# The shared network's second product in a vision transformer tower, formed transposed and turned back

## The chip, the cores and the metric

The kernel runs on one core of one Trainium2 chip. The metric is the device time in microseconds (us) of one execution; the kernel before was run three times: 559.74, 560.98 and 562.35 us, median 560.98.

## What is computed

64 images of 3 x 224 x 224 are cut into 8 x 8 patches; each patch (2352 numbers) becomes a token of 128 numbers, and each image has a class token beside its 64 patch tokens. One attention layer with 8 heads follows, then a feed-forward stage with two networks: a shared one, and eight experts of which two are chosen per token. All of it is in float32. The stage the change is about, cut to what matters:

```
flat = layernorm(h)                                  # tokens x 128
h_shared = swiglu(flat @ shared_in_w.T)              # tokens x 256
out_shared = h_shared @ shared_out_w.T + shared_out_b
h_expert = swiglu(flat @ expert_in_w.T)
routed = cnt @ expert_out_bias
for e in range(8):
    routed = routed + comb[:, e:e+1] * (h_expert @ expert_out_weight[e].T)
return h + (out_shared + routed)
```

## The kernel before

The images are worked on in eight groups of eight, so a group has 512 patch tokens (`TOK`), in four tiles of 128 (`TILES`). The 64 class tokens make one small group of their own at the end (`GROUPS`, 64 rows). Five programs, one for each engine, are written out by hand, and run in that order on their engine; they meet in semaphores (`need` waits for a count, `then_inc` adds to it). The order of the work is therefore the order of the code.

TensorE's body for group g does four things in turns. It runs the attention of group g; it multiplies out the patches of group g+1 into the PSUM bank `acc` (`fill`, L410, eighteen products with 128 rows and a last one, L415, with 48 rows); it turns the new tokens of g+1 into rows (`to_natural`, into bank C1); and it runs the feed-forward stage of group g-1 (`ffn_in`, `counts`, `shared_out`, `expert` 0 to 7). Groups 1 to 6 have all of this; group 0 has no group before it, and group 7 none after it, so that its body has an order of its own. After the eight bodies comes a tail: the feed-forward stage of group 7 (called L), and of the class tokens.

The shared network's second product for one tile of 128 tokens is `shared_out` (L564 to L577): the tile's columns of `hidden` are the stationary operand, the 128 columns of `w_sout` stream through, two such products (256 hidden numbers) are summed, and a third adds the biases (stationary `count_t`, 9 rows: eight expert counts and a one; streaming `out_bias`). The sum stands in bank C0 with tokens on the partitions. A float32 product is two instructions on TensorE in the trace, each with a weight load of its own.

In the body of groups 1 to 6 the order near it is: `prob_transpose(3)`, the last patches and L415, `shared_out` of tiles 0 and 1, `prob_v(3)` (the last product of the attention, L497), `to_natural`, `shared_out` of tiles 2 and 3, `expert` 0, `attn_transpose`, `expert` 1, `out_proj`, `expert` 2, `normed_t`, `expert` 3 to 5, `z_transpose` (L396 with z_nat), `expert` 6 and 7. `expert(g-1, 0)` writes bank C1 and waits for `nat_done`, which is ScalarE's copy of the new tokens out of C1. `z_transpose` waits for `z_done`, VectorE's last step of the second layernorm.

VectorE's body goes, from the end of `prob_v(3)` on: `attn_scale(1)` (L1099), `attn_sum(1)` (L1113), `norm1` of g+1 (L1004 to L1017; its power is done by GpSimd, L1442), `shared_add` (L1217, which waits for the shared product), `norm1_scale`, `weigh` 0, `residual` (L1119), `norm2` (power by GpSimd, L1446), `weigh` 1, `norm2_scale` (L1021, four instructions that write z_nat), and the other `weigh`s (L1233). ScalarE's body copies PSUM to SBUF (`probs_out`, `counts_out`, `natural`, `attn_out`, `normed_t`), all through the helper at L796.

## Time and profile before

| what | value |
|---|---|
| the runs | 559.74, 560.98, 562.35 us |
| span of the profiled execution | 562.2 us |
| its own time | not listed apart; the highest of the runs is 562.35 us |
| TensorE busy | 502.9 us, 89% of the span |
| weight loads busy | 353.4 us, 63% |
| VectorE busy | 335.3 us, 60% |
| ScalarE busy | 179.7 us, 32% |
| GpSimd busy | 183.0 us, 33% |
| TensorE's mean granted clock | 0.923 |

The span is the time from the first to the last instruction of one execution. TensorE is by far the busiest engine, but a busy share is an average over stages: what counts is the chain of waits, which starts at the last instruction and goes back at each step to what released it. In the profile's lists a matmul stands as out<-streaming operand, stationary operand; a line such as L396 or L796 is that of a helper, so that the tile's name says which step it is. The PEclk row of the page is the granted clock in 40 slices of 14 us, in tenths (9 is 90% or more).

### The profile page before, as it was taken

The numbers are of one execution on the slowest core, as the hardware profiler recorded it, in microseconds if no ns is written. First come the engines' busy times: TensorE is split into PE (matmuls) and PEld (weight loads), VectorE is DVE, ScalarE is ACT, GpSimd is POOL, SyncE is SP. The second block draws the span as 40 slices with busy tenths as digits, with TensorE's granted clock in tenths as the row PEclk, the third lists the DMA queues.
The fourth block names the chain that finished last, engine by engine and source line by source line (L and its number), as shares of the span: only waits on it lengthen the run. The fifth ranks groups of instructions, "written<-read, shape, count | busy, mean of one in ns | idle before, by whom it ended". The sixth has DMA issues, their size and how long they took to land.

```text
span 562.2 us, 7098 instructions
## 1 busy us (share of the span) xinstructions
PE 502.9 (89%) x2241; PEld 353.4 (63%) x2241; DVE 335.3 (60%) x867; ACT 179.7 (32%) x334; POOL 183.0 (33%) x214
## 2 busy tenths in 40 slices
PE   5596885999999999999999999999999968698775
PEld 2244543855875587558755876587658756596563
DVE  0042358274776477647764777577756768935672
ACT  0015215342174216421642164216421652002320
POOL 6000006221271128112811182118211825226235
PEclk9788696599999999999999999999999998758988
DMA  8954150036004510451045104510000000000000
GB/s 342 366 179 175 45 187 1 0 112 211 22 0 131 193 41 1 132 179 53 0 131 174 57 0 129 172 61 1 20 1 0 2 19 1 0 1 1 18 2 21
DMA packets 14413, 44.71 MB, mean 80 GB/s; under 512 B 1721, under 2 KB 7090, under 8 KB 14386
## 3 DMA queue, kind: packets, MB, share of 16 engines
q1 hardware_dynamic: 12882, 42.39, 22.6%
q10 hardware_dynamic: 1504, 1.99, 1.1%
q8 instruction: 14, 0.23, 0.2%
q14 instruction: 13, 0.11, 0.1%
HBM read 42.24 MB, written 2.13 MB: 79 GB/s over the span
## 4 chain that ended last, share of the span: by engine, by line
PE 65%; DVE 17%; issue 7%; DMA 4%; POOL 4%; ACT 1%; ACTq 1%; DVEq 0%; POOLq 0%; SPq 0%
PE acc L410 21%; PE scores L471 6%; PE O L497 5%; PE B L396 4%; DMA bq_row<-in_bq_row 3%; DVE z_nat L1021 3%; PE acc L629 2%; DVE stats L1004 2%; PE B L453 2%; PE acc L415 2%; PE C L547 1%; POOL rstd L1446 1%; PE C L574 1%; DVE attn_nat L1113 1%; PE scores L549 1%
## 5 line engine op out<-in xcount | busy, mean ns | idle before, releaser
L410 PE MATMUL acc<-x_main,w_patch 128*128 128x512 f32 x288 | 141.4, 619 | 5.9 <-DMA w_patch<-in_w_patch 5.9
L410 PEld LDWEIGHTS acc<-x_main,w_patch 128*128 128x128 f32 x288 | 54.7, 200 | 50.3 <-issue 42.0
L1509 POOL TENSOR_TENSOR prod<-prod 128x512 f32<-128x512 f32 (+1 forms) x33 | 42.6, 1291 | 33.3 <-DVE prod L1233 33.3
L796 ACT ACTIVATE probs<-shift 128x512 f32<-128x512 f32 x32 | 20.4, 638 | 83.5 <-DVE shift L1073 83.5
L1502 POOL TENSOR_TENSOR hidden_lo<-silu,hidden_hi 128x512 fp32r<-128x512 f32 (+1 forms) x18 | 20.9, 1163 | 76.8 <-ACT hidden_hi L796 76.7
L497 PEld LDWEIGHTS O<-v_bd,probs_t 128*128 128x128 f32 x256 | 32.4, 195 | 21.2 <-ACT probs_t L796 11.9
L471 PE MATMUL scores<-k_bd,q_mask 128*128 128x260 f32 x128 | 38.9, 430 | 6.3 <-DVE shift L1073 3.1
L1069 DVE TENSOR_REDUCE row_max<-scores 128x8 f32<-128x520 f32 x32 | 22.3, 698 | 30.7 <-PE scores L471 30.3
L497 PE MATMUL O<-v_bd,probs_t 128*128 128x64 f32 (+1 forms) x256 | 35.4, 283 | 5.6 <-ACT probs_t L796 5.6
L1461 POOL TENSOR_TENSOR p_cls<-exp_cls,row_rec 128x16 f32<-128x16 f32 x16 | 5.4, 337 | 104.5 <-DVE row_rec L1088 100.0
L1442 POOL TENSOR_TENSOR rstd<-var,neg_half 128x4 f32<-128x4 f32 x8 | 8.1, 1015 | 87.0 <-DVE var L1017 87.0
L471 PEld LDWEIGHTS scores<-k_bd,q_mask 128*128 128x128 f32 x128 | 23.6, 205 | 19.0 <-DVE shift L1073 7.9
L796 ACT ACTIVATE probs_t<-B 128x512 f32<-128x512 f32 x32 | 19.0, 593 | 50.8 <-PE B L396 50.8
L1099 DVE TENSOR_TENSOR attn_patch<-O,row_rec 64x256 f32<-64x256 f32 x32 | 13.5, 422 | 32.4 <-PE O L497 31.9
L1021 DVE TENSOR_SCALAR z_nat<-h,mv,rstd 128x128 f32<-128x128 f32 (+1 forms) x33 | 28.8, 929 | 5.5 <-POOL rstd L1446 5.5
L1233 DVE TENSOR_TENSOR prod<-scores,comb 128x512 f32<-128x512 f32 (+1 forms) x33 | 22.6, 683 | 15.1 <-POOL routed L1516 9.8
L1233 DVE TENSOR_TENSOR prod<-C,comb 128x512 f32<-128x512 f32 (+1 forms) x33 | 22.0, 680 | 14.3 <-PE C L602 14.3
L600 PE MATMUL C<-w_eout_hi,hidden_hi 128*128 128x512 f32 (+1 forms) x66 | 29.2, 442 | 0.0
L600 PE MATMUL scores<-w_eout_hi,hidden_hi 128*128 128x512 f32 (+1 forms) x66 | 28.7, 435 | 0.0
L601 PE MATMUL C<-w_eout_lo,hidden_hi 128*128 128x512 f32 (+1 forms) x66 | 27.4, 415 | 0.0
L602 PE MATMUL C<-w_eout_hi,hidden_lo 128*128 128x512 f32 (+1 forms) x66 | 27.3, 413 | 0.0
L1511 POOL TENSOR_TENSOR prod<-prod 128x256 f32<-128x256 f32 (+1 forms) x33 | 26.2, 794 | 2.6
(239 smaller groups left out, 1052.6 us busy)
## 6 DMA issues: line engine op xcount, KB each, us to landing
x_main<-in_x_main SPq DMA_DIRECT2D x48, 768.0 KB, 4.2
out_tokens<-y_out SPq DMA_DIRECT2D x16, 128.0 KB, 2.5
w_patch<-in_w_patch ACTq DMA_DIRECT2D x6, 192.0 KB, 12.0
prod<-in_w_eout SPq DMA_DIRECT2D x2, 512.0 KB
x_tail<-in_x_tail SPq DMA_DIRECT2D x8, 96.0 KB, 3.1
silu<-in_w_in SPq DMA_DIRECT2D x2, 256.0 KB
hidden<-in_rows ACTq DMA_DIRECT2D x1, 256.0 KB, 14.9
w_attn<-in_w_attn ACTq DMA_DIRECT2D x1, 256.0 KB, 16.9
```

Source lines behind the costliest of these rows:

```text
L396: last = nc.tensor.transpose(dst[0:rows, t * 128:(t + 1) * 128], src, ident)
L410: last = mm(acc[:, :], w_patch[:, j, :], x_main[:, j, :], start=(j == 0), stop=False)
L471: last = mm(scores[:, b2, 0:HP * SEQ], q_mask[:, b, :, :].rearrange("p e n -> p (e n)"), k_bd[:, b, :, :].rearrange("p h m -> p (h m)"), s ...
L497: last = mm(O[:, c:c + 64], probs_t[p % 2][:, hp * 128:(hp + 1) * 128], pair, start=True, stop=True)
L600: mm(dst[0:rows, :], h_hi, w_hi, start=(c == 0), stop=False)
L601: mm(dst[0:rows, :], h_hi, w_lo, start=False, stop=False)
L602: last = mm(dst[0:rows, :], h_lo, w_hi, start=False, stop=(c == HC - 1))
L796: return nc.scalar.activation(dst, src, func, **kw)
L1021: v.tensor_scalar(dst[0:rows, t * 128:(t + 1) * 128], src[0:rows, t * 128:(t + 1) * 128], mv[0:rows, 0, t:t + 1], rstd[0:rows, t:t + 1], A ...
L1233: v.tensor_tensor(prod[t % 2][0:rows, half, :].rearrange("p (e d) -> p e d", d=D), src[0:rows, :].rearrange("p (e d) -> p e d", d=D), bcas ...
L1509: q.tensor_tensor(p[r, 0, :], p[r, 0, :], p[r, 1, :], ALU.add).then_inc(tree1_done.sem, 1)
L1511: q.tensor_tensor(p[r, 0, 0:2 * D], p[r, 0, 0:2 * D], p[r, 0, 2 * D:4 * D], ALU.add)\
```

## The change

The shared product of a group is formed once, the other way round: `w_sout` is stationary and the 512 tokens of `hidden` stream. The result stands with features on the partitions, in bank C0. ScalarE copies it to SBUF (into `hn_t`, under the name `ysh_t`), and TensorE turns it back into C0 with four transposes, from which VectorE reads as before. For the class tokens 64 columns stream, in another part of bank B0. Two events are new (`sht_full`, `sht_done`). The places of the steps move as well.

```
@@ banks
         def shared_bank(g):
+            return B0[:, 384:512] if is_class(g) else C0
+
+        def shared_t_bank(g):
             return B0[:, 256:384] if is_class(g) else C0
+
+        ysh_t = hn_t
@@ TensorE
-            def shared_out(g, t, rows, final):
-
-                if t == 0:
-                    need(pe, hid_done, g)
-                    need(pe, cnt_done, g)
-                cols = slice(t * 128, t * 128 + rows)
-                dst = shared_bank(g)[0:rows, t * D:(t + 1) * D]
+            def shared_t(g, n):
+
+                need(pe, hid_done, g)
+                need(pe, cnt_done, g)
+                dst = shared_t_bank(g)[:, 0:n]
                 for c in range(HC):
-                    mm(dst, hidden[:, c, cols], w_sout[:, c, :], start=(c == 0), stop=False)
-                last = mm(dst, count_t[:, cols], out_bias[:, :], start=False, stop=True)
-                if final:
-                    last.then_inc(sh_full.sem, 1)
+                    mm(dst, w_sout[:, c, :], hidden[:, c, 0:n], start=(c == 0), stop=False)
+                mm(dst, out_bias[:, :], count_t[:, 0:n], start=False, stop=True).then_inc(sht_full.sem, 1)
+
+            def shared_natural(g, tiles, rows):
+
+                need(pe, sht_done, g)
+                for t in range(tiles):
+                    last = nc.tensor.transpose(shared_bank(g)[0:rows, t * D:(t + 1) * D], ysh_t[:, t * 128:t * 128 + rows],
+                                               ident)
+                last.then_inc(sh_full.sem, 1)
@@ TensorE, the body (not nxt is group 7)
                 if not nxt:
-                    shared_out(g - 1, 0, 128, False)
-                    shared_out(g - 1, 1, 128, False)
-                    shared_out(g - 1, 2, 128, False)
+                    shared_t(g - 1, TOK)
                 prob_v(g, 2)
                 fill(14, 18)
                 prob_transpose(g, 3)
                 fill(18, NMAIN + 1)
                 if nxt and last:
-                    shared_out(g - 1, 0, 128, False)
-                    shared_out(g - 1, 1, 128, False)
+                    shared_t(g - 1, TOK)
                 elif not nxt:
-                    shared_out(g - 1, 3, 128, True)
+                    shared_natural(g - 1, TILES, 128)
                     expert(g - 1, 1, 128)
                 prob_v(g, 3)
                 if nxt:
                     to_natural(g + 1)
                 if nxt and last:
-                    shared_out(g - 1, 2, 128, False)
-                    shared_out(g - 1, 3, 128, True)
                     expert(g - 1, 0, 128)
+                    shared_natural(g - 1, TILES, 128)
@@ TensorE, the tail
-            for t in range(TILES):
-                shared_out(L, t, 128, t == TILES - 1)
+            shared_t(L, TOK)
...
             gates(GROUPS, 1, IMAGES)
+            shared_natural(L, TILES, 128)
             for u in range(1, 4):
                 expert(L, u, 128)
...
             expert(L, 6, 128)
+            shared_t(GROUPS, IMAGES)
             expert(L, 7, 128)
-            shared_out(GROUPS, 0, IMAGES, True)
+            shared_natural(GROUPS, 1, IMAGES)
             expert(GROUPS, 0, IMAGES)
@@ ScalarE
+            def shared_out(g, n):
+                need(act, sht_full, g)
+                if is_class(g):
+                    need(act, sh_full, g - 1)
+                go(ysh_t[:, 0:n], shared_t_bank(g)[:, 0:n]).then_inc(sht_done.sem, 1)
...
                 probs_out(g, 2)
                 if nxt and last:
                     counts_out(g - 1, TOK)
+                elif not nxt:
+                    shared_out(g - 1, TOK)
                 probs_out(g, 3)
+                if nxt and last:
+                    shared_out(g - 1, TOK)
                 if nxt:
                     natural(g + 1, 1 - par)
...
             route_exp(L, TILES, 128)
+            shared_out(L, TOK)
...
             counts_out(GROUPS, IMAGES)
+            shared_out(GROUPS, IMAGES)
```

In the listings below a line of the helper or of a step has moved by a few numbers in the kernel after: L574 and L575 become L578 and L579, the transposes back are L585, L497 is L503, L396 is L402, and L600 is L610. On TensorE, in the body of groups 1 to 6 from L415 to the transposes of attn_nat, before:

```order
L415 MATMUL acc<-x_tail,w_patch_tail 128x512 [waits x_in6]
L574 MATMUL C0<-w_sout,hidden 128x128 [waits cnt_done,hid_done]
L574 MATMUL C0<-w_sout,hidden 128x128
L575 MATMUL C0<-out_bias,count_t 128x128
L574 MATMUL C0<-w_sout,hidden 128x128 x2
L575 MATMUL C0<-out_bias,count_t 128x128
L497 MATMUL O<-v_bd,probs_t1 128x64 [waits pt_done]
```

And there after:

```order
L421 MATMUL acc<-x_tail,w_patch_tail 128x512 [waits x_in6]
L578 MATMUL C0<-hidden,w_sout 128x512 [waits cnt_done,hid_done]
L578 MATMUL C0<-hidden,w_sout 128x512
L579 MATMUL C0<-count_t,out_bias 128x512
L503 MATMUL O<-v_bd,probs_t1 128x64 [waits pt_done]
L503 MATMUL O<-v_bd,probs_t1 128x64 x3
L402 MATMUL C1<-const,h_t 128x128 [waits hid_done,hT_done]
L402 MATMUL C1<-const,h_t 128x128 x3
L610 MATMUL C1<-w_eout_hi,hidden_hi 128x512 [waits nat_done,hlo_done]
```

Ahead of the attention's last product stand three products of 512 columns where six of 128 stood, and the first expert product follows directly on the transposes whose copy it waits for. On TensorE at the end of the tail, from the last instruction of group L's expert product 7 to the first of the class tokens' expert products, before:

```order
L602 MATMUL C<-w_eout_hi,hidden_lo 128x512
L574 MATMUL B<-w_sout,hidden 64x128 [waits cnt_done,hid_done]
L574 MATMUL B<-w_sout,hidden 64x128
L575 MATMUL B<-out_bias,count_t 64x128
L600 MATMUL C<-w_eout_hi,hidden_hi 64x512 [waits prod_done,hlo_done]
```

And the shared product after, from the last instruction of group L's expert product 6 to the first of its product 7:

```order
L612 MATMUL scores<-w_eout_hi,hidden_lo 128x512
L578 MATMUL B<-hidden,w_sout 128x64 [waits cnt_done,hid_done]
L578 MATMUL B<-hidden,w_sout 128x64
L579 MATMUL B<-count_t,out_bias 128x64
L610 MATMUL C<-w_eout_hi,hidden_hi 128x512 [waits prod_done]
```

The class tokens' shared product has moved from behind group L's last expert product to ahead of it; its transpose back stays behind (`shared_natural(GROUPS, 1, IMAGES)` in the diff).

## Rows read from the trace of the kernel before

**Rows 1.** The page: granted clock in 40 slices, in tenths.
```profile
PEclk9788696599999999999999999999999998758988
```

**Rows 2.** Chain of waits, group 4's stretch: start us, us, what.
```profile
251.40 1.05 PE acc L415 x2
252.46 0.64 PE C L574 x4
253.10 0.41 PE C L575 x2
...
254.56 1.05 PE O L497 x8
...
267.37 1.69 DVE z_nat L1021 x3
...
269.10 0.65 PE B L396 x4
...
299.04 2.57 PE acc L410 x6
301.61 0.44 PE B L396 x4
```

**Rows 3.** Timeline of TensorE, same stretch: start, us, line, out<-in [idle before <-releaser].
```profile
269.10 0.65 PE L396 MATMUL B<-const,z_nat 128*128 128x128 f32 x4 [0.76 <-DVE z_nat L1021]
...
309.09 0.71 PE L574 MATMUL C<-w_sout,hidden 128*128 128x128 f32 x4
...
311.20 1.10 PE L497 MATMUL O<-v_bd,probs_t 128*128 x8
...
314.60 0.50 PE L600 MATMUL C<-w_eout_hi,hidden_hi 128*128 128x512 f32 x1
...
316.10 0.60 PE L396 MATMUL B<-const,attn_nat 128*128 128x128 f32 x4
```

**Rows 4.** Groups of instructions, whole span: count | busy us, mean ns | idle us <-releaser.
```profile
L396 PE MATMUL B<-const,z_nat 128*128 128x128 f32 x28 | 4.6, 287 | 4.6 <-DVE z_nat L1021 4.6
```

**Rows 5.** Timeline of ScalarE, the new tokens' copy.
```profile
312.79 0.60 ACT L796 ACTIVATE h_nat<-C 128x512 f32<-128x512 f32 x1 [4.04 <-PE C L396]
```

**Rows 6.** Timeline of VectorE, from the attention's last product on.
```profile
260.84 1.11 DVE L1021 TENSOR_SCALAR hn_nat<-h_nat,mv,rstd 128x128 f32<-128x128 f32 x4 [0.40 <-POOL rstd L1442]
...
266.13 2.91 DVE L1021 TENSOR_SCALAR z_nat<-h,mv,rstd 128x128 f32<-128x128 f32 x4 [0.54 <-POOL rstd L1446]
...
312.35 0.87 DVE L1099 TENSOR_TENSOR attn_patch<-O,row_rec 64x256 f32<-64x256 f32 x2 [2.39 <-PE O L497]
...
316.44 0.69 DVE L1217 TENSOR_TENSOR y_out<-C,h 128x512 f32<-128x512 f32 x1
```

**Rows 7.** Timeline of TensorE, group 7 and an earlier slow stretch.
```profile
59.11 1.97 PE L497 MATMUL O<-v_bd,probs_t 128*128 128x64 f32 x8 [1.93 <-ACT probs_t L796]
...
467.66 1.10 PE L497 MATMUL O<-v_bd,probs_t 128*128 128x64 f32 x8 [1.35 <-ACT probs_t L796]
...
469.61 1.94 PE L471 MATMUL scores<-k_bd,q_mask 128*128 128x260 f32 x4
...
486.23 1.12 PE L396 MATMUL B<-const,attn_nat 128*128 128x128 f32 x4 [3.62 <-DVE attn_nat L1113]
```

**Rows 8.** Timeline of TensorE, tail.
```profile
521.42 0.50 PE L547 MATMUL C<-z_hi,w_in_hi 128*128 128x512 f32 x1 [1.65 <-DVE hidden L1209]
...
526.56 0.68 PE L574 MATMUL C<-w_sout,hidden 128*128 128x128 f32 x4 [1.63 <-ACT count_t L796]
...
530.75 0.27 PE L773 MATMUL B<-const,z_nat 64*128 64x64 f32 x1
...
552.87 0.43 PE L600 MATMUL C<-w_eout_hi,hidden_hi 128*64 128x512 f32 x1
```

**Rows 9.** Timeline of VectorE, tail.
```profile
534.72 0.69 DVE L1217 TENSOR_TENSOR y_out<-C,h 128x512 f32<-128x512 f32 x1 [3.27 <-DMA out_tokens<-y_out]
...
552.03 0.69 DVE L1233 TENSOR_TENSOR prod<-C,comb 128x512 f32<-128x512 f32 x1 [1.01 <-PE C L602]
```

More of the change, by code:

```diff
@@ L276, in vit_tower @@
         silu_done, hid_done = ev("silu_done", 4), ev("hid_done", 4)
+        sht_full, sht_done = ev("sht_full"), ev("sht_done")
         sh_full, ysh_done = ev("sh_full"), ev("ysh_done")
```

## The prediction

> **What bounds the kernel now.** I read the page first, then the chain of waits, then the timelines of TensorE, VectorE and ScalarE over one group, and last the tail. The page says TensorE, 89% busy; its clock row shows full speed in the middle slices, where groups 1 to 6 lie, and less at the start, in group 7 and near the end [rows 1]. So TensorE's work looks like the bound, and this change takes some away. The chain says more. In the stretch of a group it runs on TensorE through the patches and L415, then through the shared products of tiles 0 and 1 (L574, L575) to the attention's last product, L497; there it leaves TensorE, goes through VectorE and GpSimd to z_nat, and comes back at the transposes of z_nat [rows 2]. TensorE's own timeline has the mark of it: 0.76 us idle before those transposes, released by VectorE [rows 3]. The same wait stands in each of groups 1 to 6, the six together 4.6 us [rows 4]. It is TensorE's only idle time in such a group, which takes 56.6 us (L497 from 254.56 to 311.20 [rows 2, 3]).
>
> So between the end of L497 and the transposes of z_nat the layernorm chain is last, and what TensorE does there (shared products of tiles 2 and 3, six expert products) has 0.76 us of slack. What stands ahead of L497 has none. Work taken out behind L497 gains nothing; work added ahead of it costs in full.
>
> **Ahead of L497, groups 1 to 6.** Removed: the products of tiles 0 and 1. Each tile is four instructions of L574 and two of L575, 0.64 + 0.41 us, so 2 x 1.05 = 2.10 us [rows 2]. Added: the whole of the transposed product, two products with 128 rows and one with 9, each two instructions with 512 streamed columns. In float32 six such instructions of L410 take 2.57 us, 0.43 each [rows 2]. That is the low end: 2.57, or +0.47 us. The last product has few rows, and the nearest row for that is L415, with 48: its two instructions take 1.05 instead of 0.86 us [rows 2]. With it the sum is 4 x 0.43 + 1.05 = 2.77 us, or +0.67; I take this one. I see no end below zero: no float32 row of 512 columns at full clock is shorter than 0.43.
>
> The Trainium skill ("TensorE: Matmul & The Clock Gate", section "Why this matters for your kernels") says a single product with 32 rows takes the time of one with 128. By this rule the added part is 2.57 us and the step +0.47; the trace disagrees for 48 rows, 1.05 against 0.86, and I go by the trace.
>
> L497 thus ends 0.67 us later. Behind it VectorE's sequence begins with attn_patch, for which VectorE idled 2.39 us until L497 was done [rows 6], so it starts 0.67 later too, and from there to z_nat it idles only for GpSimd's two powers, 0.40 and 0.54 us, which depend on VectorE itself [rows 6]. z_nat, and with it TensorE's transposes, come 0.67 us later. Behind them TensorE has no idle time up to the next L415, so the delay stays. Six groups: 4.0 us (2.8 at the low end).
>
> **Behind L497.** TensorE loses tiles 2 and 3 (2.0 us) and gains four transposes, 0.44 us [rows 2]. It also gets a wait. expert 0 writes bank C1 and needs ScalarE's copy h_nat. Before, the copy started 1.59 us after L497's start and took 0.60 [rows 3, 5], ending at 313.39, and expert 0 came at 314.60 [rows 3]: hidden behind tiles 2 and 3. Counted from 309.09: L497 now starts at 2.77, the copy ends at 2.77 + 1.59 + 0.60 = 4.96, and expert 0, otherwise ready at about 4.15, waits some 0.85 us; it starts at 5.0 instead of 5.5. Its product takes 1.5, the transposes back 0.4, so the transposes of attn_nat start near 6.95, before at 7.01 [rows 3]. So of 1.6 us taken out here next to nothing is left, and it wouldn't count either: TensorE reaches z_nat as before and waits 0.76 + 0.67 + 0.05, about 1.5 us.
>
> Other waits stay covered. The new copy on ScalarE (0.6 us) starts at about 2.9 and is done at 3.5; queued behind it is h_nat, not ready before 4.36. VectorE's y_out, which needs the transposes back, is reached at 316.44 [rows 6], which is 7.35, now 8.0; they are done near 7.2. Were that cover gone, each late us would go straight into the z_nat chain. No DMA is added or moved.
>
> **Group 7.** Three shared products before prob_v(2) (3.15 us) become one of 2.77; the fourth becomes transposes. TensorE is done about 1 us earlier, but then waited 3.62 us for attn_nat [rows 7], behind GpSimd and VectorE, whose inputs here don't change. Nothing gained or lost.
>
> **The tail.** Group L: shared products from 526.56 to 530.75, 4.19 us [rows 8], become 2.77 + 0.44. The 1.0 us saved ends at y_out, which waits for the store of the last output until 534.72 [rows 9]: nothing. Class tokens: their shared product, before in the shadow between expert 7 and the class's expert products, now stands ahead of expert 7. VectorE multiplies expert 7 out from 552.03 for 0.69 us [rows 9], and the class's first expert product, at 552.87 [rows 8], waits for that, so it was due anyway at 552.8. With X for the six instructions of 64 columns it now starts at 552.8 + X. By L497, also 64 columns: eight take 1.05 us in the chain [rows 2] and 1.97 in a stretch at the low clock level, 1.2 GHz [rows 7]; X is 0.8 at full clock and 1.5 at the low one. The place is where the clock comes back up (1.97 and 1.05 mark the levels; the last two slices of the page stand at 8 [rows 1]); I take X = 1.2. From there the chain goes on unchanged to the end.
>
> **Sum.** 6 x 0.67 + 1.2 = 5.2 us; ends 2.8 + 0.8 = 3.6 and, with 0.1 more per group for joints between instructions and X at 1.5, 4.6 + 1.5 = 6.1. The profiled span is 562.2, giving 567.4. The span lies 1.2 us above the median of the runs, 560.98, so for the median I predict 566.2 us, and 564.6 to 567.1 if the mechanism holds.
>
> **Rivals.**
> The clock falls (slower still). In group 7 a wait of 1.35 us is followed by score products of 1.94 us instead of about 1.1 [rows 7], low clock. If the wait for z_nat, now 1.5 us, did this in six groups for some 3.3 us each, it would cost 1.65 x 6, about 10 us: 576. Against it: waits of 1.65 and 1.63 us in the tail, after which L547 and L574 run at full length (0.50 and 0.68 for four) [rows 8], while in group 7 the page shows the clock at 5 to 8 tenths over four slices, not after one wait alone [rows 1]. 6%.
>
> VectorE's chain gives (faster). z_nat's four instructions take 2.91 us where hn_nat's four of the same shape take 1.11 [rows 6]; GpSimd is adding expert products at that moment. If the later start pulled the two apart, the chain would shorten by 1.80 - 0.67 = 1.13 us and TensorE, with 0.76 us of wait, would be last: -0.8 x 6 + 1.2, near 557.5. It decides from the point where z_nat falls to less than 1.5 us. Against it: GpSimd's start hangs on the same VectorE instructions, so they move together. 6%.
>
> Streaming is cheap (faster). If the 512-column instructions ran at the pace of expert products, six in 1.50 us (316.10 - 314.60) [rows 3], the step would be -0.6 and the time 560.98 - 3.6 + 1.2 = 558.6. But those have another operand type; every float32 row says 0.43. 2%. The Trainium skill ("TensorE: Matmul & The Clock Gate", section "Back-to-back issue gap") gives about 81 ns for 128 columns and 131 ns for 512; as an estimate from that page the twelve instructions removed would be 0.97 us and the six added 0.79, a gain of 0.18 per group. The trace has 0.175 and 0.43 us per instruction.
>
> The delay is absorbed: L497 is late but something between it and z_nat has slack that I overlooked, and only the tail pays: 562.2, no change. Against it is the continuous chain. 8%.
>
> **Chances.** Forecast 78%, the others as above. What a measurement can tell from no change is 0.5%, 2.8 us. Within the forecast's 78% its low end (564.6) is clear of 563.8, but both terms a little smaller would reach it: 3% to "same". Slower 0.81, same 0.11, faster 0.08. The range 562.0 to 568.5 leaves out the clock and the faster cases and holds the rest.
>
> **What would show it.** In the changed profile: the six shared instructions in 2.6 to 2.8 us; expert 0 idle 0.7 to 1.0 us for h_nat; 1.3 to 1.6 us idle before the transposes of z_nat in six groups; a group period of 57.3 to 57.4 us; TensorE's busy time lower though the span is longer; the class's first expert product about 1.2 us later after VectorE's last product of L. Wrong if the idle time at z_nat stays at 0.76, or the clock row drops below 9 in the middle.

## The result, and the profile after

The changed kernel is slower, and by more than I predicted.

| | before | after |
|---|---|---|
| median, us (first comparison, 4 runs each) | 561.66 (559.74 to 565.00) | 570.87 (568.35 to 571.92) |
| ratio, 95% interval | | 1.0143 [1.0091, 1.0195] |
| the same kernel compared again (6 runs; 13 of before) | 563.23 | 571.43, ratio 1.0128 [1.0077, 1.0179] |
| profiled execution: span, granted clock | 562.2, 0.923 | 566.5, 0.920 |
| TensorE busy in the span | 502.9 | 498.0 |
| mean group period, groups 1 to 6 (L415, now L421, of group 1 to that of group 6, divided by 5) | 56.60 | 57.86 |

TensorE does 4.9 us less work and the program takes about 8 us longer, so the lost time is waiting, or work at the low clock. The page shows where to look: the engine and clock rows.

```profile
PE 498.0 (88%) x2130; PEld 339.3 (60%) x2130; DVE 335.2 (59%) x867; ACT 184.6 (33%) x343; POOL 183.5 (32%) x214
PEclk9797795799999989998999899999998988958998
```

Against [rows 1] the clock row now has single eights among the nines of the middle slices, where groups 1 to 6 lie. Next the chain of waits, group 4 (start us, us, what), which answers to [rows 2]; the rows there, from 251.40 on, are of the body one earlier, group 3, and group 4 of before starts at 308.04.

```profile
309.51 1.05 PE acc L421 x2
310.57 1.91 PE C L578 x4
312.48 1.05 PE C L579 x2
313.53 1.05 PE O L503 x8
...
324.65 1.02 POOL rstd L1465
...
326.94 1.70 DVE z_nat L1040 x3
328.68 0.65 PE B L402 x4
```

The chain has the shape that I predicted. From the end of L421 (310.57) to the start of L503 (313.53) lie 2.96 us, where before two shared products took 2.10. The six instructions were forecast at 2.77. TensorE's own timeline (start, us, line, out<-in [idle before <-releaser]) of the same group:

```profile
313.46 1.10 PE L503 MATMUL O<-v_bd,probs_t 128*128 x8
314.40 0.61 PE L402 MATMUL C<-const,h_t 128*128 128x128 f32 x4
315.79 0.77 PE L610 MATMUL C<-w_eout_hi,hidden_hi 128*128 128x512 f32 x1 [0.78 <-ACT h_nat L803]
316.35 0.63 PE L611 MATMUL C<-w_eout_lo,hidden_hi 128*128 128x512 f32 x1
...
318.48 0.78 PE L585 MATMUL C<-const,hn_t 128*128 128x128 f32 x4
319.10 0.60 PE L402 MATMUL B<-const,attn_nat 128*128 128x128 f32 x4
...
328.68 0.65 PE L402 MATMUL B<-const,z_nat 128*128 128x128 f32 x4 [0.64 <-DVE z_nat L1040]
```

And group 5:

```profile
373.84 0.47 PE L610 MATMUL C<-w_eout_hi,hidden_hi 128*128 128x512 f32 x1 [0.78 <-ACT h_nat L803]
374.14 0.40 PE L611 MATMUL C<-w_eout_lo,hidden_hi 128*128 128x512 f32 x1
...
375.33 0.60 PE L585 MATMUL C<-const,hn_t 128*128 128x128 f32 x4
375.76 0.60 PE L402 MATMUL B<-const,attn_nat 128*128 128x128 f32 x4
...
386.09 0.66 PE L402 MATMUL B<-const,z_nat 128*128 128x128 f32 x4 [1.39 <-DVE z_nat L1040]
```

Both groups wait 0.78 us at expert 0 for ScalarE's h_nat. In group 5 the six expert instructions behind the first are then 0.40 us long and start 0.24 apart. In group 4 they are 0.63 long and 0.43 apart. The granted clock of those stretches, by windows (us, then busy time of PE, PEld, DVE, ACT, POOL, the granted clock, DMA share, GB/s), says why:

```profile
312.00:316.00 4.00, 3.22 (x17) 1.84 (x16) 1.23 (x4) 1.19 (x2) 0.00 (x0) 0.93 0.26 106
316.00:320.00 4.00, 4.00 (x16) 3.23 (x17) 3.07 (x15) 0.27 (x1) 1.01 (x1) 0.64 0.00 0
320.00:330.00 10.00, 9.36 (x48) 7.42 (x47) 9.03 (x26) 1.55 (x3) 3.58 (x5) 1.00 0.00 0
...
370.00:374.00 4.00, 3.22 (x17) 1.80 (x16) 1.18 (x4) 1.19 (x2) 0.00 (x0) 1.00 0.26 105
374.00:378.00 4.00, 4.00 (x24) 3.40 (x24) 3.37 (x16) 0.60 (x1) 1.01 (x1) 1.00 0.00 0
```

In group 4 TensorE drops to its lower level, 1.2 GHz, at the wait for h_nat and is back at 2.4 GHz before 320: the granted shares of the two windows, 0.93 and 0.64, place the low stretch from 315.4 to 318.9. Such a stretch, beginning in the wait or at most 0.5 us behind it, stands in four of the six groups of this profile (2, 3, 4 and 6) and in five of six in the second profile of the same kernel (1, 2, 3, 5 and 6). The low stretch makes expert 0 and the transposes back (L585) late, and VectorE's timeline in group 4 shows what that hits:

```profile
314.61 0.87 DVE L1118 TENSOR_TENSOR attn_patch<-O,row_rec 64x256 f32<-64x256 f32 x2 [3.25 <-PE O L503]
...
319.40 0.69 DVE L1236 TENSOR_TENSOR y_out<-C,h 128x512 f32<-128x512 f32 x1 [0.73 <-PE C L585]
...
322.04 0.69 DVE L1138 TENSOR_TENSOR h<-B,h_nat 128x512 f32<-128x512 f32 x1 [0.33 <-PE B L518]
...
325.71 2.92 DVE L1040 TENSOR_SCALAR z_nat<-h,mv,rstd 128x128 f32<-128x128 f32 x4 [0.51 <-POOL rstd L1465]
```

Two waits stand there that [rows 6] doesn't have: y_out for the transposes back, 0.73 us, and the residual h for the output projection, 0.33. VectorE reaches y_out at 318.67 and the transposes' result comes 0.73 later; in group 5 neither wait exists. From the start of L421 (of L415 before) to the z_nat transposes it is 17.75 to 17.78 us in each group before, 18.60 in the groups where the clock held (367.49 to 386.09 in TensorE's timeline), and 19.24 (309.44 to 328.68) to 19.42 where it fell. The row that answers to [rows 4], over the whole span, hides this, since in the groups with the low clock TensorE itself is late and waits only 0.64:

```profile
L402 PE MATMUL B<-const,z_nat 128*128 128x128 f32 x28 | 4.6, 287 | 5.4 <-DVE z_nat L1040 5.4
```

5.4 us of wait against 4.6 looks like 0.8 us lost. Idle time of an engine isn't the delay of the chain: the delay is read from anchor to anchor.

In group 7 the wait for attn_nat is 4.46 us instead of 3.62 [rows 7], so the earlier end gained nothing, as predicted. At the tail, TensorE against [rows 8] and VectorE against [rows 9]:

```profile
553.36 0.95 PE L578 MATMUL B<-hidden,w_sout 128*128 128x64 f32 x4
554.24 0.48 PE L579 MATMUL B<-count_t,out_bias 9*128 9x64 f32 x2
554.64 0.50 PE L610 MATMUL C<-w_eout_hi,hidden_hi 128*128 128x512 f32 x1
...
557.19 0.41 PE L610 MATMUL C<-w_eout_hi,hidden_hi 128*64 128x512 f32 x1 [0.77 <-DVE prod L1252]
```

```profile
556.36 0.69 DVE L1252 TENSOR_TENSOR prod<-C,comb 128x512 f32<-128x512 f32 x1 [2.07 <-PE C L612]
```

The class tokens' product occupies TensorE from 553.56 (the end of the last L612 ahead of it) to 554.72 (554.24 + 0.48), 1.16 us ahead of expert 7, and the class's first expert product then waits for VectorE: the predicted X of 1.2. Yet the whole stretch from L421 of group 6 to the end takes 141.8 us, and 141.2 before. In the tail the clock differs too: twelve instructions of the class tokens' first feed-forward products, from 544.47 to 547.17 before, ran at 1.2 GHz (granted clock 0.50 in that stretch) and took 2.70 us; their like, from 549.16 to 550.62, ran at 2.4 GHz (1.00) and took 1.46. That is as much as X. Whether the change brought it or chance did, one trace of before can't say.

### The profile page after: what moved, and what is told of

It is laid out like the page before. It is cut to its first block, busy times and chain, and to the rows that moved or that the text cites. A ratio compares the mean times of both kernels' runs of the same rounds, so it can differ in the third digit from the quotient of the medians.

```text
span 566.5 us, 6886 instructions
## 1 busy us (share of the span) xinstructions
PE 498.0 (88%) x2130; PEld 339.3 (60%) x2130; DVE 335.2 (59%) x867; ACT 184.6 (33%) x343; POOL 183.5 (32%) x214
## 4 chain that ended last, share of the span: by engine, by line
PE 66%; DVE 16%; issue 8%; DMA 4%; POOL 4%; ACT 2%; ACTq 1%; POOLq 0%; DVEq 0%; SPq 0%
PE acc L416 20%; PE scores L477 6%; PE O L503 5%; PE B L402 4%; DMA bq_row<-in_bq_row 3%; DVE z_nat L1040 3%; PE acc L639 2%; PE C L578 2%; PE B L459 2%; PE acc L421 1%; DVE stats L1023 1%; PE C L553 1%; POOL rstd L1465 1%; PE C L554 1%; PE scores L553 1%
## 5 line engine op out<-in xcount | busy, mean ns | idle before, releaser
L416 PE MATMUL acc<-x_main,w_patch 128*128 128x512 f32 x288 | 139.2, 611 | 5.9 <-DMA w_patch<-in_w_patch 5.9
L503 PEld LDWEIGHTS O<-v_bd,probs_t 128*128 128x128 f32 x256 | 32.4, 196 | 26.8 <-issue 13.7
L503 PE MATMUL O<-v_bd,probs_t 128*128 128x64 f32 (+1 forms) x256 | 35.4, 283 | 6.7 <-ACT probs_t L803 6.7
L610 PE MATMUL C<-w_eout_hi,hidden_hi 128*128 128x512 f32 (+1 forms) x66 | 30.2, 457 | 5.9 <-ACT h_nat L803 4.7
L612 PE MATMUL C<-w_eout_hi,hidden_lo 128*128 128x512 f32 (+1 forms) x66 | 28.6, 434 | 0.0
L611 PE MATMUL C<-w_eout_lo,hidden_hi 128*128 128x512 f32 (+1 forms) x66 | 28.6, 433 | 0.0
L610 PE MATMUL scores<-w_eout_hi,hidden_hi 128*128 128x512 f32 (+1 forms) x66 | 28.5, 433 | 0.0
```

Source lines behind the costliest of these rows:

```text
L416: last = mm(acc[:, :], w_patch[:, j, :], x_main[:, j, :], start=(j == 0), stop=False)
L503: last = mm(O[:, c:c + 64], probs_t[p % 2][:, hp * 128:(hp + 1) * 128], pair, start=True, stop=True)
L610: mm(dst[0:rows, :], h_hi, w_hi, start=(c == 0), stop=False)
L611: mm(dst[0:rows, :], h_hi, w_lo, start=False, stop=False)
L612: last = mm(dst[0:rows, :], h_lo, w_hi, start=False, stop=(c == HC - 1))
```

## The experiments

The theory after the result: (1) in every group the transposed product delays L503, and all that follows to z_nat, by 0.83 us; (2) the 0.78 us wait at expert 0 lets the clock fall in most groups, and the low stretch costs 0.65 to 0.8 us more on the chain, through the waits of y_out and of the residual; (3) the tail costs 1.16. Rivals: it is all (1) with dearer instructions and the clock is a companion; or it is the clock alone; or the z_nat wait, not the one at expert 0, brings it down.

Every ratio is against the kernel before, run beside it on the same chip (its medians there were 561.7 to 564.4). "Clock" counts groups 1 to 6 with a low stretch; it comes from one trace of each kernel, two of the changed one.

| kernel | median us | ratio [95%] | group period | clock |
|---|---|---|---|---|
| before | | | 56.60 | 0 |
| after, first and again | 570.87, 571.43 | 1.0143, 1.0128 | 57.86, 57.99 | 4, 5 |
| fill_copy | 566.77 | 1.0065 [1.0036, 1.0094] | 57.42 | 0 |
| fill_norm | 566.87 | 1.0064 [1.0034, 1.0095] | 57.42 | 0 |
| turn_first | 570.48 | 1.0120 [1.0074, 1.0167] | 58.34 | 3 |
| bias_later | 558.74 | 0.9910 [0.9872, 0.9947] | 56.19 | 0 |
| no_bias | 559.91 | 0.9949 [0.9919, 0.9979] | 56.17 | 0 |
| product_late | 556.28 | 0.9871 [0.9818, 0.9925] | 55.65 | 0 |
| old_late | 559.86 | 0.9952 [0.9919, 0.9985] | 56.48 | 0 |
| old_early | 576.48 | 1.0242 [1.0196, 1.0287] | 59.00 | 1 |
| class_old | 569.27 | 1.0099 [1.0067, 1.0131] | 57.99 | 5 |
| late_class | 554.80 | 0.9852 [0.9808, 0.9896] | 55.67 | 0 |
| turn_attn_first | 552.99 | 0.9819 [0.9774, 0.9863] | 55.21 | 0 |

**again: the changed kernel itself**, unedited, for its spread and a second trace.

> The changed kernel once more, unedited. Theory A (the transposed product ahead of the attention's last product delays the z_nat chain by about 0.85 us in each of groups 1 to 6, and the wait of expert 0 for h_nat lets TensorE's clock fall in some of these groups, 0.65 to 0.8 us each; the class tokens' product costs 1.15 us in the tail): 6 to 10 us slower than before, with the spread of its runs wider than one group's 0.8 us, since the number of groups in which the clock falls differs from run to run. Rival B (only the delay of the chain counts, and the two profiles differ by chance): 5 to 6 us slower in every run.

Measured: 1.0128, and the clock falls in five groups instead of four. So the low stretches are no accident of one profile, and in which groups they come is not fixed by the program alone.

**turn_first: the four transposes back ahead of expert 0**, to put work into its wait.

```diff
                 if nxt and last:
-                    expert(g - 1, 0, 128)
                     shared_natural(g - 1, TILES, 128)
+                    expert(g - 1, 0, 128)
```

> The changed kernel with the four transposes back put ahead of expert 0 in groups 1 to 6, so that they fill part of its wait for h_nat. Theory A: the wait of expert 0 shrinks from 0.78 us to about 0.35, the clock stays at full speed in groups 1 to 6, y_out never waits, and each group takes 57.4 to 57.5 us; 5 to 6 us slower than before. Rival C (the clock falls because the float32 products with few rows and the transposes ahead do little work, not because of the wait): it falls as often as in the changed kernel, 8 us slower than before. Rival B: no difference to the changed kernel.

Measured: 1.0120, no faster than after, where 5 to 6 us above before were expected. The wait at expert 0 shrinks to 0.34 us and the clock holds there, but the z_nat wait grows to 1.73 to 1.77, and 0.8 to 1.6 us after it the clock falls in every second group. So the third rival holds in this kernel. TensorE's timeline of group 1:

```profile
142.80 0.47 PE L610 MATMUL C<-w_eout_hi,hidden_hi 128*128 128x512 f32 x1 [0.34 <-ACT h_nat L803]
...
155.04 0.66 PE L402 MATMUL B<-const,z_nat 128*128 128x128 f32 x4 [1.76 <-DVE z_nat L1040]
...
156.21 0.40 PE L612 MATMUL scores<-w_eout_hi,hidden_lo 128*128 128x512 f32 x1
...
157.11 0.63 PE L612 MATMUL scores<-w_eout_hi,hidden_lo 128*128 128x512 f32 x1
```

The periods alternate, 59.07, 57.41, 59.06, 57.39, 58.78 us. Against the same groups of fill_copy, below, whose clock held, a low stretch costs 1.53 to 1.57 us here, close to the 1.65 that the prediction gave its clock rival. The low stretch of the kernel after costs about half of it, since part of expert 0's delay falls into time in which VectorE is busy anyway.

**fill_copy and fill_norm: one unused product in a wait**, two instructions into the free bank acc: in fill_copy ahead of expert 0; in fill_norm ahead of the z_nat transposes, with turn_first's exchange besides.

```diff
                 if nxt and last:
+                    mm(acc[:, :], wk[:, :], hidden[:, 0, 0:TOK], start=True, stop=True)
                     expert(g - 1, 0, 128)
```

fill_norm, besides turn_first's exchange:

```diff
+                if nxt and last:
+                    mm(acc[:, :], wk[:, :], hidden[:, 0, 0:TOK], start=True, stop=True)
                 if last:
                     z_transpose(g)
```

> The changed kernel with one float32 product of 512 columns more in each of groups 1 to 6 (two instructions, 0.86 to 0.95 us, inputs that are there anyway, into bank acc, which is free; its result isn't used), put between to_natural and expert 0, where TensorE waits 0.78 us for h_nat. Theory A2 (the idle time itself lets the clock fall: at expert 0 in the changed kernel, at z_nat where the wait there is about 1.75 us): the wait at expert 0 is gone, the wait at z_nat stays at 1.3 to 1.4 us, the clock stays up in groups 1 to 6, a group takes 57.4 us; 5 x 0.7 to 0.8 us less than the changed kernel, 6 us slower than before, although TensorE does 5.5 us more. Rival C (the long float32 products do little work by the clock's measure): more of them, and the clock falls at least as often; 8 to 9 us slower than before.

> The kernel of the run with the transposes back first (waits of 0.34 us at expert 0 and 1.75 at z_nat; the clock fell in every second group there, 1.65 us each), and the same unused product of 512 columns put right ahead of the transposes of z_nat. Theory A2: the wait at z_nat falls to 0.9 us, no group loses its clock, all take 57.4 us; 5 us less than that kernel, 5 to 6 us slower than before. Rival C: the clock falls as often or more. Rival E (the added product delays the transposes of z_nat): each group 0.9 us longer.

Measured: both 1.0065, both with the clock up in all six groups. fill_copy, group 3, TensorE (L738 is the filler):

```profile
257.82 1.02 PE L738 MATMUL acc<-hidden,w_attn 128*128 128x512 f32 x2
258.76 0.47 PE L610 MATMUL C<-w_eout_hi,hidden_hi 128*128 128x512 f32 x1
...
271.02 0.66 PE L402 MATMUL B<-const,z_nat 128*128 128x128 f32 x4 [1.42 <-DVE z_nat L1041]
```

and its clock row:

```profile
PEclk9888696699999999999999999999999988858998
```

The filler computes nothing that is used and can shorten no dependence (expert 0 starts 6.3 us after L421 in both kernels), yet it takes away about half of the loss: 1.0065 against 1.0128 and 1.0143, which is 3.5 to 4.4 us. The intervals overlap a little (up to 1.0094, and from 1.0077), and the two kernels ran on different chips. Two further numbers tell it more sharply: the period of 57.42 against 57.99 and 57.86, with no low stretch against five and four; and the mean granted clock of every run, 0.923 to 0.935 in the twelve runs of fill_copy and 0.909 to 0.923 in the ten of the changed kernel. The z_nat wait is still 1.38 to 1.42 us and did no harm. This shows (2) at its place, and it leaves (1): the period of 57.42 against 56.60, +0.82 a group with the clock at its upper level throughout.

**bias_later and no_bias: what the order and the two bias instructions cost.** bias_later issues L503 between the four weight instructions and the two of the bias, and ScalarE copies h_nat ahead of the shared product. no_bias leaves the bias instructions out.

```diff
                 if nxt and last:
-                    shared_t(g - 1, TOK)
+                    shared_t(g - 1, TOK, 0)
...
                 if nxt and last:
+                    shared_t(g - 1, TOK, 1)
                     expert(g - 1, 0, 128)
```

no_bias, in shared_t, where last is now the second weight product:

```diff
-                mm(dst, out_bias[:, :], count_t[:, 0:n], start=False, stop=True).then_inc(sht_full.sem, 1)
+                last.then_inc(sht_full.sem, 1)
```

> The changed kernel with the bias product (9 rows, two instructions) put behind to_natural in groups 1 to 6, and ScalarE's h_nat copy ahead of the shared copy. What stands ahead of the attention's last product is then four instructions, 1.9 us, where the kernel before has 2.10. Theory A: z_nat comes 0.2 us earlier than before, expert 0 doesn't wait, no fall of the clock, a group takes 56.4 us (56.6 before); six groups gain 1.2 us, the tail loses 1.15: within 1.5 us of before. Rival C: the clock falls in groups 1 to 6 all the same, since the product with few rows is still there: 2 to 4 us slower than before. Rival D (TensorE's total work bounds, so moving it does nothing): as the changed kernel, 8 us slower.

> The changed kernel without the bias product (9 rows): the shared network's bias and the experts' biases are left out of the output, everything else stands in its place. Expert 0 still waits 0.78 us for h_nat, and the wait at z_nat stays near 1.4 us, since both ends of it shift alike. Chain: the attention's last product comes 1.25 us earlier than in the changed kernel (1.05 for the two instructions, 0.2 for the joint behind them), 0.4 earlier than before, so a group whose clock stays up takes 56.2 to 56.3 us. Theory G (the clock falls at expert 0 only when the wait follows a long product with few rows): no group loses its clock; with the tail's 1.15 us less the class tokens' two instructions, 1 to 2 us faster than before. Theory H (wait and streamed float32 products together suffice): the clock falls in three or more of the six groups, 0.7 us each, and the kernel is level with before or up to 2 us slower.

Measured: 0.9910 and 0.9949, both faster than before; bias_later by 5 us, where at most 1.5 were expected. The chain of bias_later (here L579 is the weights' instruction; the split helper moved the lines) stands against the rows of after above:

```profile
306.32 1.05 PE acc L421 x2
307.38 1.91 PE C L579 x4
309.29 0.85 PE O L503 x8
```

Between L421 and L503 lie 1.91 us, and L503 itself takes 0.85 instead of 1.05. So the 9-row product costs 1.05 for itself and 0.20 in the instructions behind it, 1.25 us in all; no_bias, whose L421 to z_nat is 17.35 us against 18.60, gives the same. In no_bias, whose output lacks both biases, TensorE reads:

```profile
251.79 1.98 PE L578 MATMUL C<-hidden,w_sout 128*128 128x512 f32 x4
253.61 1.00 PE L503 MATMUL O<-v_bd,probs_t 128*128 x8
...
255.83 0.48 PE L610 MATMUL C<-w_eout_hi,hidden_hi 128*128 128x512 f32 x1 [0.78 <-ACT h_nat L803]
256.15 0.39 PE L611 MATMUL C<-w_eout_lo,hidden_hi 128*128 128x512 f32 x1
```

The same wait of 0.78 us, and the clock holds in all six groups of the trace; the mean granted clock of its twelve runs is 0.922 to 0.934, against 0.909 to 0.923 of the changed kernel. The wait alone is thus not enough.

**product_late, old_late, old_early: the same products at another place.** In product_late the transposed product stands behind L503 and the transposes of h_t, directly ahead of expert 0, and ScalarE copies h_nat first; old_late and old_early take the kernel before and put all four tiles behind or ahead of L497.

```diff
                 if nxt and last:
-                    shared_t(g - 1, TOK)
-                elif not nxt:
+                if not nxt:
...
                 if nxt and last:
+                    shared_t(g - 1, TOK)
                     expert(g - 1, 0, 128)
```

old_late, against before (old_early has all four where the first two stand now):

```diff
                 if nxt and last:
-                    shared_out(g - 1, 0, 128, False)
-                    shared_out(g - 1, 1, 128, False)
...
                 if nxt and last:
+                    shared_out(g - 1, 0, 128, False)
+                    shared_out(g - 1, 1, 128, False)
                     shared_out(g - 1, 2, 128, False)
                     shared_out(g - 1, 3, 128, True)
                     expert(g - 1, 0, 128)
```

> The changed kernel with the whole transposed product put behind prob_v(3) and to_natural in groups 1 to 6, h_nat copied ahead of the shared copy. Nothing then stands between the patches and the attention's last product. Theory A: the z_nat chain starts 2.1 us earlier than before, the idle time at the z_nat transposes (0.76 before, 0.64 to 1.4 changed) is gone, expert 0 doesn't wait, TensorE's own work is the bound: 56.65 - 0.76 - about 0.7 (24 short instructions against 6 long and 4 transposes) = 55.2 us a group, 8 to 9 us gained in six groups, 1.15 lost in the tail: 7 to 8 us faster than before. Rival D: as the changed kernel, 8 us slower.

> The kernel before, not transposed, with tiles 0 and 1 of the shared product put behind prob_v(3) and to_natural, so that all four stand there in groups 1 to 6. Theory A (the place alone): the attention's last product comes 2.1 us earlier; z_nat follows until something else in VectorE's chain is last (y_out waits for the shared product, the residual for out_proj): the idle time at z_nat falls from 0.76 us to 0.3 to 0.7, a group takes 55.9 to 56.4 us; 2 to 4 us faster than before. Rival F (the gain of the late product was the transposed form): no change to before.

> The kernel before, nothing transposed, with tiles 2 and 3 of the shared product put ahead of prob_v(3) in groups 1 to 6. It adds 2.1 us ahead of the attention's last product and leaves expert 0 waiting for h_nat, and takes nothing away. Theory A2: z_nat comes 2.1 us later, TensorE waits some 2.8 us for it, and the clock falls at that wait or at expert 0 in most groups, some 1.5 us each at z_nat: 6 x 2.1 = 12.6 us, and with the clock up to 20 us slower than before. Rival (work placed there is hidden as long as TensorE's total doesn't grow): no change.

Measured: 0.9871, 0.9952, 1.0242. The change of place, with the low stretches that go with it, is worth 15 us of the kernel after (571.43 to 556.28), and old_early, which has none of the new code, loses more than the change did. The place makes the loss, not the form: at either place the transposed form is the faster one, 1.0128 against 1.0242 ahead of L503 and 0.9871 against 0.9952 behind it. old_early, groups 3 and 4 (TensorE; the last two rows are windows, us, then busy time of PE, the granted clock, DMA share, GB/s):

```profile
262.99 0.47 PE L600 MATMUL C<-w_eout_hi,hidden_hi 128*128 128x512 f32 x1 [0.78 <-ACT h_nat L796]
...
334.05 0.66 PE L396 MATMUL B<-const,z_nat 128*128 128x128 f32 x4 [1.75 <-DVE z_nat L1021]
```

```profile
334.00:336.00 2.00, 1.95 (x9) 0.90 0.00 0
336.00:340.00 4.00, 4.00 (x12) 0.62 0.00 0
```

It has the 0.78 us wait in all six groups, and the clock held behind each of them. The one low stretch, in group 4, begins 1.5 us behind the z_nat transposes, which waited 1.75 us. Expected were a z_nat wait of 2.8 us and low stretches in most groups; both missed, and the 12.6 us of the place alone came out at 13.7. In product_late and bias_later the order of ScalarE's two copies changed too; it was not tried alone. With product_late the step ahead of L503 is gone, and still the gain is less than the 2.1 us a group that this would give: L421 to z_nat is 16.83 us, 0.94 less than before. VectorE shows the new limit:

```profile
364.20 0.69 DVE L1235 TENSOR_TENSOR y_out<-C,h 128x512 f32<-128x512 f32 x1 [1.30 <-PE C L585]
...
366.83 0.69 DVE L1137 TENSOR_TENSOR h<-B,h_nat 128x512 f32<-128x512 f32 x1 [0.31 <-PE B L518]
```

y_out now waits 1.30 us for the transposes back, in the middle of the z_nat chain. old_late gains less, 0.12 us a group, for the same kind of reason:

```profile
317.25 0.69 DVE L1118 TENSOR_TENSOR h<-B,h_nat 128x512 f32<-128x512 f32 x1 [1.91 <-PE B L512]
```

There TensorE itself is late with the output projection, L512, behind 4.2 us of shared products. This is where the transposed form is better: here 2.87 us for the product (1.82 for the four L578, 1.05 for the 9 rows) and 0.44 for the transposes back, instead of 4 x 1.05 = 4.2.

**class_old and late_class: the tail.** The class tokens' product in its old form and place, in the kernel after and in product_late.

```diff
             expert(L, 6, 128)
-            shared_t(GROUPS, IMAGES)
...
-            shared_natural(GROUPS, 1, IMAGES)
+            shared_cls()
```

> The changed kernel with the class tokens' shared product in its old form and place (behind group L's expert product 7, no copy, no transpose back). Theory A: the class's first expert product no longer waits for VectorE's last product of group L, 1.15 us less in the tail; groups 1 to 6 as in the changed kernel: 7 to 8 us slower than before. Rival: the tail's place costs nothing: as the changed kernel.

> The kernel with the whole transposed product behind prob_v(3) and to_natural, and the class tokens' product in its old form and place. Both theories' terms together: a group as in the late product's run (55.6 to 55.8 us), and 1.15 us less in the tail than that run: 8 to 9 us faster than before.

Measured: 1.0099 against 1.0128 of after, and 0.9852 against 0.9871 of product_late. The first is about 1.6 us, the second 1.1, and both lie inside the intervals. The traces show the place: the idle time of 0.77 us ahead of the class's first expert product is gone in class_old. They don't show the time: from L421 of group 6 to the end class_old takes 143.8 us and after 141.8, with other low stretches in the tail. So (3) is seen where it arises and not shown in the total.

**turn_attn_first: the version that the experiments point to.** Against product_late it has the old class product, expert 0 and the transposes back behind the transposes of attn_nat, and y_out behind the first expert's product on VectorE.

```diff
                 if nxt and last:
                     shared_t(g - 1, TOK)
-                    expert(g - 1, 0, 128)
-                    shared_natural(g - 1, TILES, 128)
...
                 attn_transpose(g)
                 if nxt and last:
-                    expert(g - 1, 1, 128)
+                    expert(g - 1, 0, 128)
+                    shared_natural(g - 1, TILES, 128)
                 out_proj(g)
                 if nxt and last:
+                    expert(g - 1, 1, 128)
                     expert(g - 1, 2, 128)
...
-                if last:
+                if not nxt:
                     shared_add(g - 1, h2[1 - par], TILES, 128)
                 if nxt:
                     norm1_scale(g + 1, 1 - par)
                 if last:
                     weigh(g - 1, 0, 128)
+                if nxt and last:
+                    shared_add(g - 1, h2[1 - par], TILES, 128)
```

> The previous kernel with two more moves in groups 1 to 6. On TensorE the transposes of attn_nat stand ahead of expert 0, and out_proj ahead of expert 1, so that the attention's output doesn't wait behind an expert product; on VectorE y_out stands behind hn_nat and the first expert product. If the 0.64 us that TensorE still waits for z_nat comes from the residual waiting for out_proj, as the late product's timeline shows (0.31 us behind L518) and y_out waiting for the transposes back (1.30 us), the wait goes and a group takes 55.0 to 55.2 us: 3 to 4 us faster than the previous kernel, 11 to 13 us faster than before. Rival: y_out or GpSimd's power takes its place and nothing more is gained.

Measured: 552.99 us (550.53 to 553.69), ratio 0.9819, the fastest of all and 10.2 us below before, a little less than the 11 to 13 expected. The interval overlaps that of late_class; the period is 55.21 us against 55.67. TensorE's wait at z_nat is nearly gone, so the next us has to come from TensorE's work:

```profile
373.12 0.66 PE L402 MATMUL B<-const,z_nat 128*128 128x128 f32 x4 [0.24 <-DVE z_nat L1047]
```

## Why the prediction was wrong, step by step

Predicted 566.2 (562.0 to 568.5), measured 570.87. The direction and the main mechanism, the delay ahead of L497, were right; of the 4.7 us that were missed, these are the steps.

- **The clock rival, put at 6%.** The prediction weighed it at one wait only, the z_nat wait ("If the wait for z_nat, now 1.5 us, did this"), and of the new wait at expert 0 it asked only whether work comes late (expert 0 "starts at 5.0 instead of 5.5"), not what the clock does. The clock fell at that wait, in four or five groups, 0.65 to 0.8 us each, about 3.2 us; fill_copy removes it and gives 3.5 to 4.4 us back by the ratios. The prediction even named the weak spot, y_out's cover of 0.8 us ("Were that cover gone, each late us would go straight into the z_nat chain"), but checked it at full clock only. The z_nat wait, 1.38 to 1.42 where the clock had held, brought no low stretch.
- **The step ahead of L497: predicted +0.67, measured +0.83 a group**, by the chain from L421 to z_nat with the clock up (18.60 against 17.77). The four instructions behind the 48-row product took 1.91 instead of 4 x 0.43 = 1.72. On the chain it makes 0.16 more a group, 1.0 us in six; the joints, 0.1 a group, stood in the upper end and not in the value. The choice of L415 as the row for the 9-row product was right: 1.05 and 1.05.
- **The baseline.** The prediction went from the span of 562.2 down to the median 560.98 of three runs, 1.2 us. Each run's time is 1.8 us above its span, so the profiled execution of before lasted 564.0, and the median of 35 later runs is 563.1. A median of three runs lay 2 us low, though in the comparison with the first four runs (561.66) only 0.7 us of that counts.
- **Right:** the wait at expert 0 (0.85 predicted, 0.78; it starts 5.3 us after the shared product, not 5.0); the z_nat wait of "about 1.5" (1.39 to 1.42 where the clock held); z_nat's four instructions unchanged at 2.92 us, so the rival that VectorE's chain gives is refuted; float32 streaming at 0.43 or more, not at the experts' pace; y_out of group L still waits 3.27 us for the store; X = 1.2 (1.16). X was partly luck: 1.2 was a choice between 0.8 and 1.5, and in this trace the clock came back in the middle of the product (granted 0.67 from 553.5 to 554.8). The forecast period of 57.3 to 57.4 is that of the clock-up groups and of fill_copy, 57.42.

Do the terms add up? Six groups at 0.83 are 5.0, four to five low stretches 3.2, the tail 1.16: 9.3 us, against 8.0 [5.1, 11.0] and 7.2 [4.3, 10.1] measured. The same sum (six times the difference in period, plus 1.16 where the class product is moved) stands above the measured difference for every kernel here: fill_copy 6.1 against 3.7, turn_first 11.6 against 6.8, old_early 14.4 against 13.7, product_late -4.5 against -7.3, turn_attn_first -8.3 against -10.2. The offset is 0.7 to 4.8 us, mostly 2 to 3.

The traces show where it lies. Up to L421 (before: L415) of group 1 all kernels do the same work, and it takes 138.0 us before, 135.4 and 137.1 in the two traces of after, and 133.8 to 138.3 in all. From there to group 6 it is 283.0 against 289.3 and 289.9, as the terms say, and the groups of before are alike (56.40 to 56.71 us each). Behind it, it is 141.2 against 141.8 and 141.9, 0.6 more, where the sum puts 2.7 (0.83 for group 6, 0.7 for its low stretch, 1.16 for the class tokens). So the sum holds inside the groups and overstates the two ends, where the clock is low for parts of group 7 and of the tail in every trace. The part of it that is chance stays open, as there is one trace of before. It doesn't touch the comparisons of periods.

Open too is what exactly brings the clock down. Shown is, at expert 0: with the 0.78 us wait behind the 9-row product of 512 columns, four or five groups in six; the wait filled, none; the wait kept without the 9-row product (no_bias), none; the wait behind 128-column shared products (old_early), none. At z_nat: waits of 1.73 to 1.78 us, three groups in six (turn_first) and one in six (old_early); waits up to 1.42 us, none. So at expert 0 it took both the product and the wait. Which property of the stretch counts was not separated, and that the same kernel loses its clock in other groups from one trace to the next says that something beside the order of the work has a part. The Trainium skill ("TensorE: Matmul & The Clock Gate", section "A second HAM failure mode: psum-queue depth-cycling") says of one bf16 kernel, whose TensorE idles briefly but often between groups of matmuls, that its clock swings between the two levels and that it pays for each return. The trace agrees, with waits of 0.78 us; that the kind of work ahead of the wait counts too, as no_bias shows, the page doesn't tell.

## What to carry to other kernels

Where one product in a row of independent ones releases a long chain on other engines, put it first: its place was worth 15 us here, the form of the product about 5. When an edit makes TensorE idle, even off the path, check every such new wait for the clock, and work out what the following work costs at 1.2 GHz and which cover that uses up. Judge delays from anchor to anchor, since the idle time at the old bottleneck can shrink while the kernel gets slower.

## What the runs showed of the hardware

- A wait of 0.78 us was followed by a stretch at 1.2 GHz (315.4 to 318.9 in the rows above) in four or five of six groups of the changed kernel and in none of no_bias and old_early. Waits of 1.38 to 1.42 us were harmless in all groups of fill_copy, and waits of 1.73 to 1.78 us were followed by a low stretch in three of six (turn_first) or in one (old_early). The length of the wait alone doesn't decide.
- Unused work, two instructions in each of six groups, made a kernel 3.5 to 4.4 us faster (ratio 1.0065 against 1.0128 and 1.0143, intervals that overlap a little).
- Two float32 instructions of 512 columns take 1.05 us with 9 or 48 rows and 0.86 with 128, and the instructions behind them take up to 0.2 us more than they do behind a product of 128 rows: L503 1.05 against 0.85, four L578 1.91 behind the 48-row product and 1.82 in product_late.
